# First attention groups prepared inside the projection stage, and a dense feed-forward in three passes over split weights

## What is computed

```python
def _L0_ffn_ref(hidden_states, ...):          # "token choice": 64 rows of each batch, 256 in all
    ...
    x = sel.reshape(S, D)
    h = _rms_norm(x, ln1_w)
    ...
    x1 = x + attn_out                          # 16 heads of 128 over the 256 rows
    h2 = _rms_norm(x1, ln2_w)
    mlp = jax.nn.silu(h2 @ w_gate) * (h2 @ w_up) @ w_down      # 512 -> 2048 -> 512
    processed = x1 + mlp
    ...

def _L1_xattn_ref(x, y, ...):                  # 16 heads of 32, 512 queries, 512 keys
    ...
    q = _ln((x @ Wq + bq).reshape(b, s1, H, HD), qn_w, qn_b)
    k = _ln(kv[..., :HD], kn_w, kn_b)
    ctx = _attn(qT, k..., v...)                # softmax over 496 keys
    ctx_dca = _attn(qT, k_dca..., v_dca...)    # softmax over the last 16
    return (ctx + ctx_dca) @ Wo + bo
```

## Time and profile before

| | us |
|---|---|
| median of 3 runs | 2368.89 (2363.28 to 2370.18) |
| profiled execution | 2366.62 |
| its span, first to last instruction | 2364.9 |
| granted PE clock, mean share of full speed | 0.918 |
| feed-forward block, first weight DMA to last product | 392.6 to 492.5 |
| projection stage | 520.2 to 724.6 |
| attention, first DMA | 726.03 |

### The profile page before, as it was taken

How to read it: one execution, slowest core, us unless ns; L and a number is a source line. 1 busy time by engine, 2 the same in 40 slices (tenths; PEclk the granted TensorE clock), 3 DMA queues, 4 the chain that set the end, 5 groups by cost and what they waited for, 6 DMA issues and landing times. The chain is left out here.

```text
span 2364.9 us, 33403 instructions
## 1 busy us (share of the span) xinstructions
PE 1979.9 (84%) x10468; PEld 1418.3 (60%) x10469; DVE 1140.2 (48%) x2204; ACT 550.3 (23%) x1158; POOL 1113.4 (47%) x552
## 2 busy tenths in 40 slices
PE   5946887968863789998799999999999999999910
PEld 3424443433321333333499999999999999999810
DVE  2564442056763657675664345445444455453300
ACT  3221222101111444543223212221222122122100
POOL 0000000003461546655035558667657788781886
PEclk9977997989985789999899999999999999999955
DMA  3052003211125256631124545445444555543999
GB/s 112 0 144 66 18 27 137 85 62 56 71 78 187 89 184 204 212 109 47 38 93 166 194 137 186 154 150 178 155 161 151 188 167 182 178 154 94 208 155 196
DMA packets 199485, 305.96 MB, mean 129 GB/s; under 512 B 16472, under 2 KB 94808, under 8 KB 199416
## 3 DMA queue, kind: packets, MB, share of 16 engines
q1 hardware_dynamic: 141624, 187.24, 24.7%
q0 software_dynamic: 21504, 50.93, 9.5%
q10 hardware_dynamic: 36288, 66.84, 8.0%
HBM read 186.42 MB, written 118.55 MB: 129 GB/s over the span
## 5 line engine op out<-in xcount | busy, mean ns | idle before, releaser
L2233 PE MATMUL psum<-e_gu_high,e_rowT_high 128*128 (+1 forms) x1272 | 426.9, 338 | 4.4 <-DVE e_gu_low L2078 2.5
L2233 PE MATMUL psum<-e_gu_low,e_rowT_high 128*128 (+1 forms) x1272 | 408.1, 323 | 0.0
L1966 ACT ACTIVATE e_silu<-psum 128x352 f32<-128x352 f32 x159 | 73.9, 465 | 846.9 <-PE psum L2238 813.9
L2233 PEld LDWEIGHTS psum<-e_gu_high,e_rowT_high 128*128 128x128 f32 x1272 | 239.8, 189 | 28.3 <-issue 23.9
L2238 PE MATMUL psum<-e_gu_high,e_rowT_low 128*128 (+1 forms) x1272 | 255.2, 322 | 0.0
L2233 PEld LDWEIGHTS psum<-e_gu_low,e_rowT_high 128*128 128x128 f32 x1272 | 240.7, 189 | 3.8
L2044 DVE TENSOR_TENSOR e_midT_low<-psum,e_midT_high 128x256 fp32r<-128x256 f32 x159 | 67.5, 424 | 317.3 <-ACT e_midT_high L1975 308.1
L2238 PEld LDWEIGHTS psum<-e_gu_high,e_rowT_low 128*128 128x128 f32 x1272 | 213.1, 188 | 0.0
L2253 PE MATMUL psum<-e_d_high,e_midT_high 128*128 (+3 forms) x477 | 187.8, 394 | 1.0 <-ACT e_midT_high L1975 1.0
L2253 PE MATMUL psum<-e_d_low,e_midT_high 128*128 (+3 forms) x477 | 188.3, 395 | 0.0
L1947 POOL DMA_INDIRECT X<-d_y,f_slots x96 | 148.1, 1543 | 83.1 <-DVE f_arena L2064 52.7
(11 more groups left out here) (344 smaller groups left out, 3754.5 us busy)
## 6 DMA issues: line engine op xcount, KB each, us to landing
d_sorted<-f_hs SPq DMA_DIRECT2D x32, 1048.0 KB, 9.5
e_row<-d_sorted ACTq DMA_DIRECT2D x125, 262.0 KB
d_y<-f_arena ACTq DMA_DIRECT2D x127, 256.0 KB
f_gu_in<-in_L_ffn_w_gate SPq DMA_DIRECT2D x32, 704.0 KB, 5.2
f_gu_in<-in_L_ffn_w_up SPq DMA_DIRECT2D x32, 704.0 KB, 5.1
f_d_in<-in_L_ffn_w_down SPq DMA_DIRECT2D x32, 512.0 KB
d_y<-f_hs SPq DMA_DIRECT2D x8, 1024.0 KB, 5.7
f_d_in<-in_L_ffn_w_down SPq DMA_DIRECT2D x32, 192.0 KB
```

The source lines that it names most:

```text
L2233: nc.tensor.matmul(bank[:, 0:M].unsqueeze(1), rowT_high[par][:, k, :], w[:, bass.ds(buffer, 1), k, at:at + M], start=(k == 0 and n == 0), ...
```

## The change

Two parts, and what they need of memory.

*Feed-forward.* The weights are loaded by piece into four raw tiles, the first two of them during the heads' attention (from SP's list at h = 2). ACT casts each piece to fp32r (`high_of`), DVE subtracts (`low_of`), and PE does a piece as 16 matmuls with the high rows on the high and low weights, then 8 with the low rows on the high weights. hT and midT are split in the same way. The raw, high and low tiles are rings of four: a load waits for the subtraction four pieces back, a cast for the product four pieces back. The loops of ACT and DVE are written out.

*Attention.* A class `Scores` takes over rows, splits, scores and maxima, with tiles that live across the two stages (`far_sbuf` takes them from the other end of the memory). In `project_heads` SP loads the rows of groups 0 and 1 after the store of batch 1; in the last batch PE turns them and does all eight score pairs of group 0, ACT and POOL split them, and DVE takes three maxima ahead of the finish of k and five behind it. `sum_squares` of k and `finish` of q move ahead of the additions of b_o in every batch, and the copy x_ctx_b goes: PE reads ctxT itself. The attention stage begins with the transposes of group 0's maxima.

```diff
+        RAW, RING, EARLY = 4, 4, 2
+        raw = [far_sbuf(nc, kept, f"b_raw{n}", [P, 4, 512]) for n in range(EARLY)]
+        raw_loaded = sems(nc, c, "b_", " ".join(f"raw{n}_loaded" for n in range(RAW)))
...
+        def load_piece(sp, p):
+            kind, n = PIECES[p]
+            cols = slice(n * 512, (n + 1) * 512)
+            src = c.dram["L0_ffn_w_" + kind]
+            src = src[cols, :] if kind == "down" else src[:, cols]
+            sp.dma_start(raw[p % RAW][:], src.rearrange("(k p) n -> p k n", p=P)).then_inc(raw_loaded[p % RAW], 16)
...
+                    if h == 2:
+                        for p in range(EARLY):
+                            load_piece(sp, p)
...
-            w_gate = sbuf(nc, stack, "b_w_gate", [P, CC, INNER])
-            w_up = sbuf(nc, stack, "b_w_up", [P, CC, INNER])
-            w_down = sbuf(nc, stack, "b_w_down", [P, INNER // P, D])
+            raw += [sbuf(nc, stack, f"b_raw{n}", [P, 4, 512]) for n in range(EARLY, RAW)]
+            high, low = [[sbuf(nc, stack, f"b_w_{part}{n}", [P, 4, 512], F32R) for n in range(RING)] for part in ("high", "low")]
...
+                for p in range(EARLY, len(PIECES)):
+                    if p >= RAW:
+
+                        sp.wait_ge(piece_low, p - RAW + 1)
+                    load_piece(sp, p)
...
+                def low_of(*pieces):
+                    for p in pieces:
+                        dve.wait_ge(piece_high, p + 1)
+                        nc.vector.tensor_tensor(low[p % RING][:], raw[p % RAW][:], high[p % RING][:].bitcast(F32), ALU.subtract).then_inc(piece_low, 1)
...
+                low_of(0, 1)
+                rms_dve(dve)
+                dve.wait_ge(hT_high_ready, 1)
+                nc.vector.tensor_tensor(hT_low[:], hT[:], hT_high[:].bitcast(F32), ALU.subtract).then_inc(hT_low_ready, 1)
+                low_of(2, 3)
+                multiply(0)
+                low_of(4)
+                low_midT(0)
+                low_of(5)
...
+                def high_of(*pieces):
+                    for p in pieces:
+                        act.wait_ge(raw_loaded[p % RAW], 16 * (p // RAW + 1))
+                        if p >= RING:
+
+                            kind, n = PIECES[p - RING]
+                            act.wait_ge({"gate": gated, "up": upped, "down": out_ready}[kind], n + 1)
+                        nc.scalar.copy(high[p % RING][:], raw[p % RAW][:]).then_inc(piece_high, 1)
...
+                high_of(0, 1)
+                rms_act(act)
+                act.wait_ge(hT_written, 1)
+                nc.scalar.copy(hT_high[:], hT[:]).then_inc(hT_high_ready, 1)
+                high_of(2, 3)
+                silus(0)
+                high_of(4)
+                copy_midT(0)
+                silus(1)
+                high_of(5, 6, 7)
...
+                def product(at, p):
+                    pe.wait_ge(piece_low, p + 1)
                     for g in range(GROUPS):
+                        rows = slice(g * P, (g + 1) * P)
                         for k in range(CC):
-                            last = nc.tensor.matmul(c.bank[at + g][:], hT[:, k, g * P:(g + 1) * P],
-                                                    w[:, k, n * 512:(n + 1) * 512], start=(k == 0), stop=(k == CC - 1))
+                            for m, w in enumerate((high, low)):
+                                nc.tensor.matmul(c.bank[at + g][:], hT_high[:, k, rows], w[p % RING][:, k, :], start=(k == 0 and m == 0), stop=False)
+                    pe.wait_ge(hT_low_ready, 1)
+                    for g in range(GROUPS):
+                        rows = slice(g * P, (g + 1) * P)
+                        for k in range(CC):
+                            last = nc.tensor.matmul(c.bank[at + g][:], hT_low[:, k, rows], high[p % RING][:, k, :], start=False, stop=(k == CC - 1))
                     return last
...
+                    pe.wait_ge(midT_low_ready, n + 1)
+                    for g in range(GROUPS):
+                        for k in range(4):
+                            last = nc.tensor.matmul(c.bank[6 + g][:], midT_low[:, g, k * P:(k + 1) * P], high[p % RING][:, k, :],
...
+                            turn_mid(n)
+                        down(n, p).then_inc(out_ready, 1)
...
+    def load_rows(self, sp, g):
+        b, hc = g // (X_H * X_HD // P), g % (X_H * X_HD // P)
+        for kind, name in enumerate(("d_xq", "d_xk")):
+            sp.dma_start(self.row[kind][:, g % 2], self.c.dram[name][b, :, hc * P:(hc + 1) * P].rearrange("(j p) d -> p j d", p=P)).then_inc(
+                self.rows_loaded[g % 2], 16)
...
+    def split(self, act, g, kind):
+        act.wait_ge(self.turned[kind], g + 1)
...
+        self.nc.scalar.copy(self.high[kind][:, g % 3, :], self.first).then_inc(self.high_ready[kind], 1)
+        if g >= 1:
+
+            act.wait_ge(self.low_ready[kind], g)
+        self.nc.scalar.copy(self.exact[kind][:], self.first).then_inc(self.exact_ready[kind], 1)
...
+        pool.wait_ge(self.high_ready[kind], g + 1)
...
+        self.nc.gpsimd.tensor_tensor(self.low[kind][:, g % 3, :], self.exact[kind][:], self.high[kind][:, g % 3, :].bitcast(F32),
+                                     ALU.subtract).then_inc(self.low_ready[kind], 1)
...
+        if n == 0:
...
+        if g * self.PAIRS + n >= 1:
+            pe.wait_ge(self.max_ready, g * self.PAIRS + n)
...
+    def find_max(self, dve, g, n):
+        j, h = n // 2, n % 2 * 2
+        dve.wait_ge(self.scored, g * self.PAIRS + n + 1)
+        banks = self.c.psum[:, self.at:self.at + 2, :]
+        to = self.nmax[g % 2][:, j, h * X_HD:(h + 2) * X_HD].rearrange("p (h e) -> p h e", e=X_HD)
+        self.nc.vector.reduce_max(to[:, :, 1], banks[:, :, S - X_LAST:S], AX.X, negate=True)
+        self.nc.vector.reduce_max(to[:, :, 0], banks[:, :, 0:S - X_LAST], AX.X, negate=True).then_inc(self.max_ready, 1)
...
+                if b == 1:
+
+                    sp.wait_ge(stored[0], 16 * 3)
+                    for g in range(2):
+                        early.load_rows(sp, g)
...
+            for b in range(B - 1):
+                power(b, 0)
+                power(b, 1)
+            power(B - 1, 0)
+            for kind in range(2):
+                early.low_part(pool, 0, kind)
+            power(B - 1, 1)
+            for kind in range(2):
+                early.low_part(pool, 1, kind)
...
+                if b == B - 1:
+
+                    dve.wait_ge(sel_loaded, 16)
+                    nc.vector.memset(early.nmax[0], 0.0)
+                    nc.vector.tensor_copy(early.sel[:], sel_in[:]).then_inc(early.sel_ready, 1)
+                    dve.wait_ge(early.sel_ready, 1)
...
+                sum_squares(b, 1)
+                finish(b, 0, q[:, par], q_scaled)
                 for j in range(JT):
 
                     t = b * JT + j
                     nc.vector.tensor_tensor(c.X[:, t, :], c.X[:, t, :], b_o[:], ALU.add)
-                sum_squares(b, 1)
-                finish(b, 0, q[:, par], q_scaled)
+                if b == B - 1:
+                    for n in range(3):
+                        early.find_max(dve, 0, n)
                 finish(b, 1, k[:, par], k_scaled)
+            for n in range(3, early.PAIRS):
+                early.find_max(dve, 0, n)
...
-                nc.scalar.copy(ctx_b[:], c.ctxT[:, b])
...
+                    if b == B - 1:
+                        for kind in range(2):
+                            early.split(act, a, kind)
...
+                    if b == B - 1 and j in (1, 2):
+                        if j == 1:
+
+                            pe.wait_ge(q_copied, B * JT)
+                        else:
+                            pe.wait_ge(early.exact_ready[0], 1)
+                        early.turn_rows(pe, 0, j - 1)
+            for n in range(early.PAIRS):
+                early.scores(pe, 0, n)
+                if n < 2:
+                    pe.wait_ge(early.exact_ready[1 - n], n + 1)
+                    early.turn_rows(pe, 1, n)
...
-            for g in range(2):
-                load_rows(g)
-            sp.dma_start(sel_in[:], c.dram["i_sel"].rearrange("p (a k) -> p a k", a=2)).then_inc(const_loaded, 16)
...
-                    load_rows(g + 2)
+                    early.load_rows(sp, g + 2)
...
-            for n in range(PAIRS):
-                find_max(0, n)
```

More of the change, by code:

```diff
@@ L831, in _ @@
[L831 to L842 removed]
+                            for m, w in enumerate((high, low)):
+                                nc.tensor.matmul(c.bank[6 + g][:], midT_high[:, g, k * P:(k + 1) * P], w[p % RING][:, k, :],
+                                                 start=(n == 0 and k == 0 and m == 0), stop=False)
@@ L1224, in context_attention @@
     PAIRS = 2 * JT
-    KINDS = ("q", "k")
+    early = c.scores
     with ExitStack() as stack:
@@ L1380, in _ @@
                 if g + 2 < GROUPS:
[L1381 removed]
+                    early.low_part(pool, g + 2, 1)
                 if g < GROUPS:
```

267 lines of the change are left out of this document (138 added, 129 removed).

## The result

The changed kernel takes 2330.5 us (median of 4 runs, 2327.2 to 2338.0), the one before 2366.9 (4 runs, 2363.3 to 2370.2): ratio 0.9851, 95% interval 0.9821 to 0.9881. The forecast was 2337 with a range of 2327 to 2349. The profiled execution took 2328.3 us, its span 2326.6: 38.3 less than before, where the sum forecast 31.6 less.

A forecast was written before the change was run, and what follows sets the result against it. TensorE was taken to bound the feed-forward, and latency the attention's start. Feed-forward -12.8 and attention -18.8 gave -31.6 on 2366.6, so 2335.0; with the median 2.3 above the profiled execution, 2337, range 2327 to 2349 us.

The forecast's parts named there:

- Pieces: Feed-forward: a piece of 24 fp32r matmuls takes 5.59 us against 6.87, so 12 pieces give -15.3 us.
- the cover: Feed-forward: casts and subtractions are ready before TensorE asks for them; price 0.
- The rival of 216 ns: Feed-forward: fp32r matmuls of 512 columns take 216 ns each, giving 2332 us in total; chance 8%.
- Start of the block: Feed-forward's start: casts and subtractions ahead of the squares delay the first product by 2.5 us.
- The head start: Attention's start: with early scores, the maxima of group 0 are turned 26.2 us earlier.
- The rows of group 2: Attention's start: these rows land 12.2 us after the stage's start, behind eleven other loads, so TensorE waits 8.0 us.
- The catch-up of 0.6: Attention's start: what follows the wait for group 2's rows recovers some 0.6 us, exponentials being done meanwhile.
- Power stretch: Projection stage: VectorE work beside GpSimd's power might lengthen it, 2.8 us over four batches at most; taken as 0.
- The split as the bound: Feed-forward rival: cast, subtraction and product follow one another, 9.8 us a piece, 2388 us in total; chance 4%.
- The head start was not given back: The rival claimed group 0's step waits for something tied to the attention's start, losing most of 18.8 us: 2356; chance 8%.

The follow-up runs named there:

- e9: Kernel after, with the pass of the weights' low part left out of every feed-forward product: 2316.0 us, ratio 0.9773 to the kernel before.
- e10: Kernel after, with each weight subtraction on VectorE made twice: 2336.1 us, ratio 0.9868 to the kernel before.
- e4: Kernel after, with the feed-forward's first two casts and subtractions put behind the squares and scaling of the rows: 2329.5 us, ratio 0.9824 to the kernel before.
- e1: Kernel before, with only the three-pass feed-forward and its two early weight loads added: 2355.2 us, ratio 0.9944 to the kernel before.
- e3: Kernel after, with the rows of group 2 loaded in the projection stage's last batch, behind the store of v: 2322.9 us, ratio 0.9803 to the kernel before.
- e5: Kernel after, with the rows of group 2 loaded at the head of the attention's load list: 2323.7 us, ratio 0.9831 to the kernel before.
- e6: Kernel after, with none of group 0's eight maxima ahead of the k finish: 2343.5 us, ratio 0.9920 to the kernel before.
- e7: Kernel after, with all eight of group 0's maxima ahead of the k finish: 2344.0 us, ratio 0.9902 to the kernel before.

## Why the prediction was right

- **Pieces.** Forecast 5.59 us by a spacing of 0.233 in the routed stage; measured 5.44, a spacing of 0.227. Twelve pieces gave 17.2 instead of 15.3; the stretch is 16.6 shorter, since the half clock at its start costs the first piece 2.2 us where it cost the old one 1.8 (the other 0.2 is open). e9 shows the slope, e10 the cover. With the start's +2.4, part 1 is worth 14.3 us by the lengths, forecast 12.8: the price of a piece was 0.15 us too high. The rival of 216 ns is refuted by the same rows: the trace doesn't reach the Trainium skill's figure (page "TensorE: Matmul & The Clock Gate", section "Wait — 56ns, not 53.3ns?") here either.
- **Start of the block.** 13.1 forecast, 13.0 measured; the chain of casts, subtractions, squares and hT was named rightly. e4 took it away.
- **The head start.** Turn of group 0's maxima 26.2 earlier by forecast, 25.4 measured. With the projection's first row turn (526.69 in the kernel before, 514.44 after) as zero, all steps of the last batch came 1.0 to 1.4 us later than forecast, from the copies (685.22 + 12.25 = 697.5 for 696.1) to the last maximum; 0.5 of it came back at the barrier, 0.9 us after the last maximum for 1.4. e1, without early scores, shows half of that lateness too (its last batch's row turn stands 129.7 us after the first, before 129.2), so it isn't all part 2's.
- **The rows of group 2.** Wait of 8.0 forecast, 7.7 measured; 12.2 us after the stage's start both times, though two terms of it were off by 0.7 to 0.8 in opposite directions: SyncE issued the k rows 7.0 us after the start, forecast 7.8, and they landed 5.1 us later, forecast 4.4. That these cancel is luck. e3 and e5 show that the cause is the list. The catch-up of 0.6 came as 0.6 (7.71 against 7.1).
- **Power stretch.** 0 forecast, 0 measured (12.52).
- **What was missing.** The forecast took all else as unchanged. It moved by -5.7 us in this trace, nearly all where the instructions are the same: the attention of heads 3.3 longer, the groups after t1 and the stretch behind the attention 7.5 shorter. The granted clock differs in each: 0.98 before and 0.93 after over 280 to 330, 0.83 and 0.90 in the groups, 0.91 and 0.95 behind the attention. That the total came so close is partly luck: such shifts reach 12 us between e9 and the kernel after, and the forecast had no term for them.
- **The split as the bound**, the rival on the other side, is refuted by e9 and e10. The head start was not given back: 18.3 us (25.4 - 7.1) stand in the kernel after, and at least as many in every trace that keeps the split of three and five maxima; e6 and e7, with another split, keep 15 and 13.

## What to carry over

Price a move in lengths between the same two instructions of each trace, and compare totals only after that: here 5 us of real gain (e4) were reversed between two profiled executions and came out of many executions only at the edge of their intervals. Work laid beside a saturated TensorE is free up to its cover, while the same work ahead of the first product costs all of its length, so put the critical chain first and the preparation behind it. When a stage starts with work already done, its loads become the next wait: move them as early as the buffer they fill is free.

## What the hardware showed unexpectedly

- **VectorE against GpSimd depends on what GpSimd runs.** The forecast said that the two don't lock each other, from the power. That holds for the power. But a GpSimd subtraction of 1.26 us stretches a VectorE pass beside it. In e6, GpSimd's row that overlaps VectorE's 3.34 us pass (699.54):

```profile
699.47 1.26 POOL L1005 TENSOR_TENSOR y_q_low<-f_gu_in,y_q_high 128x512 fp32r<-128x512 f32 x1
```

The overlap is 1.19 us and the pass is 1.06 longer than the 2.28 of such a pass elsewhere; in the kernel after the overlap with the low part of 703.51 is 0.32 and the pass is 0.19 longer (2.47); in e7, with no low part beside it, it takes 2.28. For this operation the Trainium skill's rule (page "SBUF — State Buffer", section "Who interferes with whom") agrees with the trace; for the power it doesn't. The power also reads less (128x64 for 128x512 elements), and no run tells which of the two makes the difference.
- **The granted clock differs between kernels where their instructions don't.** Kernels with the same instructions in a stretch differ by up to 9.6 us there (304.1 to 313.7), with 25.5 and 46.6 us at half clock. The attention of heads took 174.1 to 177.4 us in kernels that are identical up to its end. Two traces of the kernel after agree to 0.2 us in every length, but its executions without the profiler are up to 10.8 us apart, so a pattern read from one trace isn't sure to be that of the next execution.
